# A cross-attention kernel on one core: a reordered front, a regrouped end, and row moments of three half chunks moved to ScalarE

## The reference

```
Q = x @ wq.T + bq ; K = ctx @ wk.T + bk ; V = ctx @ wv.T + bv      # 16 heads of 16
scores = Q K^T / sqrt(16);  scores = where(mask == 0, -1e9, scores)
attn = softmax(scores)                                             # over 64 keys
out = (attn V) @ wo.T + bo + x
mu, var = mean and variance of out over its 256 columns
result = (out - mu) * rsqrt(var + 1e-5) * gamma + beta
```

## Time and profile before

| what | value |
|---|---|
| median of 3 runs | 165.4 us (164.56 to 165.82) |
| the profiled execution's own time | 164.33 us |
| its span, first to last instruction | 162.5 us |
| busy: TensorE, VectorE, GpSimd, ScalarE | 137.3, 124.9, 115.5, 94.7 us |
| mean granted TensorE clock | 0.964 |

### The profile page before, as it was taken

The page is one execution under the profiler, slowest core; times in us unless marked ns, Lnnn a source line. Parts: engine busy times, 40 slices in busy tenths (PEclk is TensorE's granted clock), DMA queues, the critical chain, the costliest instruction groups (busy, mean ns, idle before and its releaser), DMA issues.

```text
span 162.5 us, 2904 instructions
## 1 busy us (share of the span) xinstructions
PE 137.3 (84%) x992; PEld 87.0 (54%) x992; DVE 124.9 (77%) x231; ACT 94.7 (58%) x166; POOL 115.5 (71%) x111
## 2 busy tenths in 40 slices
PE   0798975989899998999899989998999579999400
PEld 0676853746556655565556565655665335468300
DVE  0263899348788897989798979898989797999951
ACT  3349687593963666766676675846763815640220
POOL 5003741029999539999999999999981899667783
PEclk9999999699999999999999999999999999999955
DMA  4988983999927886006730940048003503003024
GB/s 119 342 234 198 283 197 85 317 244 269 287 71 187 314 217 252 0 0 196 180 148 0 224 167 0 2 105 274 12 2 76 187 0 129 0 4 122 7 94 166
DMA packets 10175, 23.21 MB, mean 143 GB/s; under 512 B 1584, under 2 KB 1840, under 8 KB 10160
## 3 DMA queue, kind: packets, MB, share of 16 engines
q1 hardware_dynamic: 9584, 22.03, 46.7%
q10 hardware_dynamic: 576, 0.99, 1.9%
HBM read 14.62 MB, written 4.19 MB: 116 GB/s over the span
## 4 chain that ended last, share of the span: by engine, by line
PE 45%; DVE 15%; POOL 14%; issue 7%; DMA 7%; SPq 6%; ACT 3%; POOLq 1%; DVEq 0%
PE ps_w L436 11%; PE ps_w L357 9%; PE ps_w L331 8%; DMA m_sb<-maskT 7%; PE ps_s L385 6%; PE ps_s L412 5%; POOL y L873 5%; DVE nmax L667 4%; POOL y L876 4%; DVE turned L688 3%; SPq L215 3%; PE ps_s L391 3%; ACT y L585 2%; DVE cn L701 2%; POOL rstd L857 2%
## 5 line engine op out<-in xcount | busy, mean ns | idle before, releaser
L667 DVE TENSOR_REDUCE nmax<-ps_w 128x8 f32<-128x512 f32 x56 | 37.7, 678 | 15.2 <-PE ps_w L357 14.8
L572 ACT ACTIVATE probs<-ps_s 128x512 f32<-128x512 f32 x64 | 33.1, 602 | 18.3 <-PE ps_s L396 18.3
L810 POOL TENSOR_TENSOR xt_l<-xt_sb,xt_h 128x1024 fp32r<-128x1024 f32 x7 | 16.6, 2374 | 30.6 <-ACT xt_h L533 19.8
L436 PE MATMUL ps_w<-wo_sb,cn 128*128 128x256 f32 x112 | 29.3, 387 | 3.9 <-DVE cn L701 3.6
L357 PEld LDWEIGHTS ps_w<-k_half,q_mask 128*128 128x128 f32 x112 | 17.3, 190 | 25.5 <-DVE nmax L667 19.7
L357 PE MATMUL ps_w<-k_half,q_mask 128*128 128x256 f32 x112 | 27.9, 335 | 3.2 <-DVE nmax L667 2.9
L436 PEld LDWEIGHTS ps_w<-wo_sb,cn 128*128 128x128 f32 x112 | 19.3, 189 | 9.2 <-DVE cn L701 5.5
L585 ACT ACTIVATE y<-res,shift,rstd 128x256 f32<-128x256 f32 x28 | 14.8, 590 | 12.6 <-POOL shift L859 12.5
L873 POOL TENSOR_TENSOR y<-y,brow 128x512 f32<-128x512 f32 x14 | 17.9, 1279 | 4.5 <-ACT y L585 4.1
L688 DVE STREAM_TRANSPOSE turned<-ps_s 128x1024 f32<-128x1024 f32 x16 | 19.8, 1240 | 0.8 <-PE ps_s L412 0.8
L844 POOL TENSOR_TENSOR x_sb<-x_sb,brow 128x1024 f32<-128x1024 f32 x8 | 19.1, 2382 | 0.1
(11 more groups left out here) (75 smaller groups left out, 203.3 us busy)
## 6 DMA issues: line engine op xcount, KB each, us to landing
m_sb<-maskT SPq DMA_DIRECT2D x32, 128.0 KB, 3.5
q_mask<-mask SPq DMA_DIRECT2D x32, 128.0 KB, 2.6
x_sb<-x SPq DMA_DIRECT2D x8, 512.0 KB, 4.3
xt_sb<-xT SPq DMA_DIRECT2D x7, 512.0 KB, 4.4
out<-y SPq DMA_DIRECT2D x6, 512.0 KB, 3.4
xt_sb<-xT SPq DMA_DIRECT2D x2, 256.0 KB, 5.7
out<-xt_sb SPq DMA_DIRECT2D x2, 256.0 KB, 2.0
brow<-bias_rows SPq DMA_DIRECT2D x1, 384.0 KB, 6.4
```

Of the source, the lines that this page charges most:

```text
L436: return pe.matmul(tile_outputs(c, i)[:, t], cn[:, c % 2, j, (2 * i + t) * P:(2 * i + t + 1) * P], wo_sb[:, j], start=j == 0 and c < LAST, ...
L572: act.activation(probs[:, g % 2, quad], ps_s[:, quad], ACT.Exp).then_inc(e_done, 1)
L667: dve.tensor_reduce(nmax[:, c % 2, t].rearrange("p (q r) -> p q r", r=32)[:, :, 2 * j:2 * j + 2], max_bank(c, i).rearrange("p (q h k) -> p ...
```

## The change

On SyncE, chunk 0's mask is also loaded as m_first (two transfers of 64 partitions) in place of its m_sb load, ahead of xT 1 and wv; m_sb has three buffers now (NI); xT 3 and the last three bias rows come ahead of the mask copies of chunks 1 and 2; the copy of chunk 0 is gone. VectorE writes chunk 0's mask values straight into q_mask (`first_mask_values`), converts masks 0 and 1 after the maxima of products 4 and 5, and builds v_bd with two operations behind the third maximum of chunk 1. TensorE projects the values with 16 products of 64 partitions by 128 columns ahead of all maxima. GpSimd waits for mask 2 before `low_x(2)`, and for the bias rows only in `with_bias(0)`.

At the end, for three half chunks (`on_scalar`: both of chunk 5, the first of chunk 6), VectorE computes no moments. ScalarE sums the rows (`row_sums`), GpSimd makes nmean of it, ScalarE sums the squared deviations (`square_sums`), and GpSimd goes on. For the second half of chunk 6, gamma and beta are applied on VectorE (`gammas`, `betas`) from a PSUM copy of both. The host no longer sends batch 0 of ctx twice.

The core of the diff:

```diff
@@ -190,6 +198,14 @@
             return 4 * (c + 1) if c < LAST - 2 else 4 * (LAST - 2) + 4 * (2 * (c - LAST + 2) + second + 1)
+        def on_scalar(c, i):
+            return (c, i) in ((LAST - 2, 0), (LAST - 2, 1), (LAST - 1, 0))
+        def moments_done(c, i):
+            return 2 * sum(not on_scalar(n // 2, n % 2) for n in range(2 * c + i + 1))
@@ -209,11 +225,11 @@
             def load_mask(c):
-                if c >= 2:
-                    sp.wait_ge(mask_done, c - 1)
+                if c >= NI:
+                    sp.wait_ge(mask_done, c - NI + 1)
                 for quad in range(QUADS):
-                    sp.dma_start(m_sb[quad_rows(quad), c % 2], maskT[c].rearrange("(a k) n -> k a n", a=2)
-                                 ).then_inc(in_mask[c % 2], 16)
+                    sp.dma_start(m_sb[quad_rows(quad), c % NI], maskT[c].rearrange("(a k) n -> k a n", a=2)
+                                 ).then_inc(in_mask[c % NI], 16)
@@ -245,19 +261,20 @@
             load_first_xt(1)
+            for half in range(2):
+                sp.dma_start(m_first[rows(half)], maskT[0]).then_inc(in_mfirst, 16)
+            load_xt(1)
+            sp.dma_start(wv_sb[:], wv).then_inc(in_wv, 16)
             load_mask(0)
-            sp.dma_start(wv_sb[:], wv).then_inc(in_wv, 16)
-            load_xt(1)
-            copy_mask(0)
...
             load_mask(2)
+            load_xt(3)
+            sp.dma_start(brow[:, 1:4], bias_rows[:, 1:4].to_broadcast([P, 3, D])).then_inc(in_rows, 16)
...
             copy_mask(2)
-            load_xt(3)
             load_x(0)
-            sp.dma_start(brow[:, 1:4], bias_rows[:, 1:4].to_broadcast([P, 3, D])).then_inc(in_rows, 16)
@@ -287,18 +304,20 @@
                         mm = pe.matmul(ps_w[:, 1, j * 256:j * 256 + 256], wk_sb[:, d, j * P:(j + 1) * P],
-                                       ctx_t[:, d, 0:BATCHES], start=d == 0, stop=d == PC - 1)
+                                       ctx_t[:, d], start=d == 0, stop=d == PC - 1)
...
-            def project_values(b):
-                if b == 0:
-                    pe.wait_ge(in_wv, 16)
-                for d in range(PC):
-                    mm = pe.matmul(value_bank(b)[:, 0, (b % 2) * 256:(b % 2) * 256 + 256],
-                                   ctx_t[:, d, b:b + 2].rearrange("p b k -> p (b k)"), wv_sb[:, d],
-                                   start=d == 0, stop=d == PC - 1)
-                mm.then_inc(v_done, 1)
+            def project_values():
+                pe.wait_ge(in_wv, 16)
+                for b in range(BATCHES):
+                    for d in range(PC):
+                        for h in range(2):
+                            mm = pe.matmul(projected_values(h)[:, b], ctx_t[:, d, b],
+                                           wv_sb[:, d].rearrange("p (q e) -> p q e", e=32)[:, :, 16 * h:16 * h + 16],
+                                           start=d == 0, stop=d == PC - 1)
+                            if d == PC - 1:
+                                mm.then_inc(v_done, 1)
@@ -338,7 +357,10 @@
                 if i == 0:
-                    pe.wait_ge(mk_in[c % 2], 16 * QUADS * (c // 2 + 1))
+                    if c == 0:
+                        pe.wait_ge(mfirst_done, 2)
+                    else:
+                        pe.wait_ge(mk_in[c % 2], 16 * QUADS * (c // 2 + c % 2))
@@ -585,6 +604,23 @@
+            def row_sums(c, i):
+                k = 2 * (c - LAST + 2) + i
+                act.wait_ge(res_done, 2 * c + i + 1)
+                if k:
+                    act.wait_ge(square_done, 2 * k)
+                for t in (2 * i, 2 * i + 1):
+                    act.activation(unused[:, t], res[:, c % 2, t], ACT.Copy, accum_out=row_sum[:, c % 2, t:t + 1]
+                                   ).then_inc(sum_done, 1)
+            def square_sums(c, i):
+                k = 2 * (c - LAST + 2) + i
+                act.wait_ge(sum_done, 2 * k + 2)
+                act.wait_ge(ln_done, deviations_done(c, i == 1) - 3)
+                for t in (2 * i, 2 * i + 1):
+                    act.activation(unused[:, t], res[:, c % 2, t], ACT.Square, bias=nmean[:, c % 2, t:t + 1],
+                                   accum_out=square_sum[:, c % 2, t:t + 1]).then_inc(square_done, 1)
@@ -593,8 +629,8 @@
             identity_rows(0)
+            high_x(1)
             first_queries_out(0)
-            high_x(1)
@@ -620,23 +656,30 @@
                 if s == LAST:
-                    normalised(LAST - 2, (0, 1))
+                    square_sums(LAST - 2, 0)
...
                 if s == LAST:
+                    normalised(LAST - 2, (0, 1))
+                    row_sums(LAST - 2, 1)
+                    square_sums(LAST - 2, 1)
+                    row_sums(LAST - 1, 0)
                     normalised(LAST - 2, (2, 3))
+                    square_sums(LAST - 1, 0)
...
                     negative_max(s + 1)
+                if s + 1 == LAST:
+                    row_sums(LAST - 2, 0)
...
             act.wait_ge(div_done, GROUPS)
-            act.activation(beta(), brow[:, 3], ACT.Copy).then_inc(beta_done, 1)
+            act.activation(ps_s[:, 1].rearrange("p (n d) -> p n d", d=D), brow[:, 2:4], ACT.Copy).then_inc(gb_done, 1)
             normalised(LAST - 1, (2, 3))
-            act.wait_ge(bet_done, 2 * LAST)
+            act.wait_ge(dve_bet_done, 1)
@@ -717,16 +759,18 @@
                     dve.wait_ge(ln_done, deviations_done(c - 2, True))
+                if on_scalar(c, i):
+                    return
...
                                  ).then_inc(bn_done, 1)
-                dve.wait_ge(bn_done, 2 * n)
+                dve.wait_ge(bn_done, moments_done(c, i))
...
                 c = LAST
-                dve.wait_ge(mv_done, TILES * c + 2 * i + 2)
+                dve.wait_ge(mv_done, moments_done(c, i))
@@ -735,21 +779,40 @@
                 dve.wait_ge(ln_done, deviations_done(LAST - 1, True) + 2 * (i + 1))
-                dve.wait_ge(beta_done, 1)
+                dve.wait_ge(gb_done, 1)
...
                 for t in (2 * i, 2 * i + 1):
-                    dve.scalar_tensor_tensor(y_of(c)[:, t], y_of(c)[:, t], rstd[:, c % 2, t:t + 1], beta(),
+                    dve.scalar_tensor_tensor(y_of(c)[:, t], y_of(c)[:, t], rstd[:, c % 2, t:t + 1], gamma_beta(1),
...
+            def gammas():
+                two = y[:, (LAST - 1) % 2, 2:4]
+                dve.wait_ge(y_done, TILES * LAST)
+                dve.tensor_tensor(two, two, gamma_beta(0).unsqueeze(1).to_broadcast([P, 2, D]),
+                                  ALU.mult).then_inc(dve_gam_done, 1)
+            def betas():
+                two = y[:, (LAST - 1) % 2, 2:4]
+                dve.wait_ge(dve_gam_done, 1)
+                dve.tensor_tensor(two, two, gamma_beta(1).unsqueeze(1).to_broadcast([P, 2, D]),
+                                  ALU.add).then_inc(dve_bet_done, 1)
+            def first_mask_values():
+                dve.wait_ge(in_mfirst, 32)
+                for half in range(2):
+                    r = rows(1 - half)
+                    dve.tensor_scalar(q_mask[r, 0, half], m_first[r].unsqueeze(1).to_broadcast([64, 2, CHUNK]), 0.0, -BIG,
+                                      ALU.is_equal, ALU.mult).then_inc(mfirst_done, 1)
             def mask_values(c):
-                dve.wait_ge(in_mask[c % 2], 16 * QUADS * (c // 2 + 1))
-                dve.tensor_scalar(mask[:, c % NM], m_sb[:, c % 2], 0.0, -BIG,
+                dve.wait_ge(in_mask[c % NI], 16 * QUADS * (c // NI + 1))
+                dve.tensor_scalar(mask[:, c % NM], m_sb[:, c % NI], 0.0, -BIG,
...
             first_low_x()
-            mask_values(0)
+            first_mask_values()
@@ -758,10 +821,9 @@
                 maxima(0, i)
-                if i == 3:
-                    mask_values(1)
+                if i in (4, 5):
+                    mask_values(i - 4)
             mask_values(2)
-            value_blocks()
@@ -771,6 +833,8 @@
                     moments(s - 2, 1)
+                elif s == 0:
+                    value_blocks()
@@ -794,11 +858,13 @@
             moments(LAST, 0)
+            moments(LAST, 1)
             centred(0)
-            moments(LAST, 1)
+            centred(1)
             scaled(0)
-            centred(1)
+            gammas()
             scaled(1)
+            betas()
@@ -840,6 +906,8 @@
             def with_bias(c):
+                if c == 0:
+                    pool.wait_ge(in_rows, 16)
@@ -847,7 +915,24 @@
                 n = deviations_done(c, tiles.stop == TILES) - 4
-                pool.wait_ge(mv_done, TILES * c + tiles.stop)
+                second = int(tiles.stop == TILES)
+                if on_scalar(c, second):
+                    k = 2 * (c - LAST + 2) + second
+                    pool.wait_ge(y_done, TILES * (c - 1))
+                    pool.wait_ge(sum_done, 2 * k + 2)
+                    pool.tensor_scalar(nmean[:, i, tiles], row_sum[:, i, tiles], -1.0 / D, 0.0, ALU.mult, ALU.add
```

(42 more changed lines are left out.)

23 lines of the change are left out of this document (13 added, 10 removed).

## The result

| kernel | median of all runs | ratio to before |
|---|---|---|
| before | 164.98 us (163.84 to 165.82) | |
| the change | 168.55 us (166.99 to 171.51) | 1.0196, 95% interval 1.0115 to 1.0276 |

The change is 2% slower. Its profiled execution took 166.99 us with a span of 164.8, against 164.33 and 162.5.

What follows compares the result with a forecast made beforehand. The prediction took a serial GpSimd/ScalarE chain to bound the end, with TensorE pacing the middle. The end's 6.5 us and the front's 0.4 us summed to 6.9 us slower, forecast as 171.4 us, range 167.5 to 174.

Steps and rivals of the forecast that it cites:

- y of chunk 5, 3.8 us and a 0.3 us gain ahead: At the end, first-half y goes behind the second exponentials, costing 3.8 us; last scores come 0.3 us sooner.
- The turn, 6.9 us: Each of two GpSimd/ScalarE turns at the end lengthens from 5.5 to 6.9 us, with squares between nmean and veps.
- Behind the last turn, 9.9 us to the store: From y of chunk 6's first half at 156.6, through GpSimd and then VectorE's gamma and beta, to the store at 166.5.
- The end in total: The store goes out at 166.5 in place of 160.05, so the end costs 6.5 us.
- The front, a loss of 0.4 us: In the front, chunk 1's third product starts at 28.2 instead of 27.80, behind late mask copies: 0.4 us lost.
- between 20.4 + 4.0 + 2.4 = 26.8 and 28.1: Landing time of chunk 1's mask copies, queued behind mask 2, xT and bias rows; 27.0 was taken.
- the first rival: Front gain survives: copies land at 24.6, third product at about 25.8, 3.5 us gained; 167.5 us, chance 0.14.
- the prediction's own last sentence: Wrong if the chain's end runs through TensorE or VectorE, or chunk 1's first product starts before 25 us.
- The likeliest case: End costs 6.5 us and front loses 0.4: 171.4 us, chance 0.68.
- The faster rival: VectorE's queue holds back the end, so three moment pairs less bring 2.8 us: 161.5 us, chance 0.04.

Runs made afterwards that it cites:

- e4: e3 with y of chunk 5's first half moved behind the second exponentials, as in the change: 165.92 us, ratio 1.0011 to before.
- e9: e8 with three more projection-sized TensorE products, their result overwritten, ahead of the first turn: 160.58 us, ratio 0.9733 to before.
- e3: The change with all moments back on VectorE and y of chunk 5's first half ahead of the second exponentials: 161.37 us, ratio 0.9687 to before.
- e1: Only the front of the change, with the end of the kernel before: 162.83 us, ratio 0.9752 to before.
- e2: Only the end of the change, with the front of before (narrower value products and smaller ctx load kept): 171.21 us, ratio 1.0207 to before.
- e5: The change with chunk 5's first-half moments on VectorE and its y ahead of the second exponentials: 165.02 us, ratio 1.0013 to before.
- e6: e3 with x of chunks 0, 1 and 2 loaded ahead of chunk 1's mask copies: 167.15 us, ratio 1.0134 to before.
- e7: e3 with xT 3 and the bias rows behind chunk 1's mask copies: 161.33 us, ratio 0.9791 to before.
- e8: e3 with masks 0 and 1 converted one maximum earlier each: 161.0 us, ratio 0.9753 to before.
- e10: e8 with GpSimd's deviations of chunk 5's first half ahead of its bias addition for chunk 7: 160.6 us, ratio 0.9713 to before.
- e11: e8 unchanged, run again on the chip of e9 and e10: 160.76 us, ratio 0.9744 to before.

## Why the prediction was right, and where it was not

The direction and the bound of the end were right: slower, by the GpSimd/ScalarE chain. The size was too large: 171.4 forecast, 168.55 measured; from the profiled execution 6.9 us more were expected, 2.7 came.

- *y of chunk 5, 3.8 us and a 0.3 us gain ahead.* Right in the main. y stands 9.1 us behind the turn of chunk 7 (139.99 - 130.86) against 5.1 (139.01 - 133.87); e4 gives 4.0 for this alone. Of the 0.3 ahead less than 0.1 came: from the last product of maxima to the turn it is 1.45 us (129.41 to 130.86), where it was 1.52 (132.35 to 133.87).
- *The turn, 6.9 us.* Measured 6.5, twice. The squares with their handover took 1.17 (144.05 to 145.22), not 1.4, and from gamma to nmean it was 2.6, not 2.73. 0.4 too much in each turn.
- *Behind the last turn, 9.9 us to the store.* Measured 9.4 (152.99 to 162.35). The two new operations on VectorE took 0.68 each (the last stands at 161.64), not 0.8, and each next one begins a tenth before the busy time of the last ends.
- *The end in total.* 6.5 forecast; 5.2 measured from the last product of maxima.
- *The front, a loss of 0.4 us.* Wrong in sign: 2.9 gained by the last product of maxima. The step that failed is "between 20.4 + 4.0 + 2.4 = 26.8 and 28.1". Mask 2's last load had landed at 19.6, not 20.4 to 21.7, and xT and bias rows took 2.2 us behind it, not the 4.0 that the prediction took from x and the rows. DMA issues of 15.6 to 16 us and 22 to 22.8 us in the changed profile:

```profile
brow<-bias_rows SPq DMA_DIRECT2D x1, 384.0 KB, 6.1
...
q_mask<-mask SPq DMA_DIRECT2D x2, 128.0 KB, 2.4
...
15.68 0.43 SPq L274 DMA_DIRECT2D brow<-bias_rows  x1
20.20 5.28 SPq L245 DMA_DIRECT2D q_mask<-mask  x8
```

The rows issued at 15.68 had landed by 21.8, 2.6 us before the earliest time that the prediction allowed (24.4). From 21 to 21.5 us next to nothing moved (12 GB/s), and each copy landed 2.3 to 2.5 us after its issue. So the copies met an empty queue and took their own 2.65 + 1.9 us. Why 896 KB took 4.0 us in the earlier trace rows and 2.2 here no run shows; it is not fixed. In e9's execution the rows landed at 24.5 and chunk 1's first product started behind the copies at 26.8, which is the forecast's front, and in the eight other traces with this order the rows landed between 21.3 and 23.0. The prediction took one sample for the rule.

What ran is the first rival's case, "The copies land soon after their issue", which had a chance of 0.14. By the prediction's own last sentence it was a sign of being wrong: chunk 1's first product started at 24.90, before 25. The rival has the third product at 25.8; it is seen at 26.48 here and at 26.04 in e3. Its full 3.5 us need a clock that stays up. In the changed execution the stretch of lower clock moved ahead, over the scores of chunk 0: 1.69 and 1.88 us (22.00 and 22.67) for what takes 1.14 and 1.04.

The likeliest case was therefore right in the end and wrong in the front. Both errors made it too slow, by 1.3 and 3.3 us. The direction held because the end costs more than the front gains. That the median lies in the range, 167.5 to 174, is owed to the first rival, whose sum is the lower bound; the profiled execution, 166.99, lies below even that. The faster rival was excluded rightly: in e3, with all its moments on VectorE, GpSimd never waits for them.

## What to carry to other kernels

Where the end is one chain that goes back and forth between two in-order queues, work moved to one of them counts in full if the chain then crosses once more, and what it pushes behind itself in that queue can cost more than the work (here 4.0 us for a place, 1.05 for a crossing). Relieving an engine that is near the bound but not on the chain gave nothing here. And a transfer time read from one row is one sample: the same bias rows landed at 21.3 to 24.5 us in nine executions with the same order of loads. Ask for the moment at which the next transfer comes how much stands in the queue, and take a range from several executions.

## What the runs showed of the hardware

- A row sum on ScalarE is two instructions. Two lines' instructions in the changed profile (ns, shortest, median, longest):

```profile
L613 ACT ACTIVATE unused<-res x6: 399/412/426, 132.0 to 145.7; 128x256 f32<-128x256 f32 x6
L613 ACT ACTIVATION_READ_ACCUMULATOR unused<-res x6: 185/192/211, 132.4 to 146.0; 128x1 f32 x6
...
L621 ACT ACTIVATE unused<-res,nmean x6: 491/507/529, 135.3 to 151.0; 128x256 f32<-128x256 f32 x6
```

A tile of 256 columns costs 0.41 us as a plain sum and 0.51 as a square with a bias from memory, and the read-out (0.19) begins 0.1 us before the sum's busy time ends: two tiles took 0.9 us as sums and 1.1 as squares, no more than two tiles of y without a sum (1.09).
- The sixteen value products of 64 partitions by 128 columns, alternating between the two halves of the array, took 1.97 us (11.38 to 13.35), about half of what the eight full ones of 256 columns took (12.52 to 15.27 and 16.13 to 17.16, 3.8 us). Both are 2048 columns in all and both ran at the full clock, so the reading that fits is that the two halves ran at the same time; no run tests it by itself.
- The lower clock of TensorE (1.2 GHz) came for one stretch in the front (before, the change, e1, e2, e5, e6, e7, e9), for one between 124 and 132 us (e8, e10, e11) or nowhere between 11 and 151 us (e3, e4), in kernels that are nearly equal. No run shows what brings it. One stretch of the changed profile: its length, the busy times by engine, then the granted clock, 0.50 of full speed, the DMA engines' share and GB/s:

```profile
22.46:25.88 3.42, 3.42 (x24) 2.03 (x16) 0.15 (x1) 1.16 (x3) 1.93 (x1) 0.50 0.95 202
```

It costs 1 to 1.5 us where it falls on TensorE's work, as much as several of the edits: six products take 2.90 in place of 1.40.
